# Two pairs of PSUM banks instead of one for the down projection of a mixture-of-experts layer, on 8 cores

## The reference

```
logits = xf @ w_gate                       # [8192, 8]
top_logits, top_idx = top_k(logits, 2)
weights = softmax(top_logits)
for each expert e, its tokens:
    inter = silu(x @ wi_0[e]) * (x @ wi_1[e])   # [tokens, 1024]
    y     = inter @ wo[e]                       # [tokens, 2048]
out = sum over the two experts of a token, weighted
x = x + out
```

## Time and profile before

| | us |
|---|---|
| median of 3 runs | 6443.39 |
| the three runs | 6667.94, 6424.47, 6443.39 |
| the profiled execution, its own time | 6424.47 |
| its span (slowest core, core 7) | 6423.4 |
| spans of the other cores | 6388.9 to 6421.0 |

### The profile page before, as it was taken

One profiled execution on the slowest core, in us unless ns is written; L12 is line 12 of the kernel. 1 busy time (PEld: TensorE's weight loads), 2 busy tenths in 40 slices (PEclk: granted clock), 3 DMA queues, 4 the chain that ended last, 5 costly groups with the idle time before them and its releaser, 6 DMA issues.

```text
span 6423.4 us, 39888 instructions; the slowest of 8 cores (6388.9 to 6423.4 us)
## 1 busy us (share of the span) xinstructions
PE 3070.6 (48%) x13620; PEld 1334.4 (21%) x13620; DVE 887.8 (14%) x1577; ACT 889.7 (14%) x2498; POOL 0.2 (0%) x4
## 2 busy tenths in 40 slices
PE   0002053063063063053437774334448888888887
PEld 0001021021021021021213332111113333333333
DVE  1111101101101101101010002331111111111111
ACT  1001003012022021021041003431110000000000
POOL 0000000000000000000000000000000000000000
PEclk9999575575575575575758885556769999999999
DMA  6764623524524514525310111113332111111111
GB/s 187 246 215 157 222 98 131 201 94 150 197 79 160 199 72 171 182 85 171 137 66 27 53 53 46 40 60 122 120 135 107 66 66 59 59 66 66 61 60 77
DMA packets 181570, 732.71 MB, mean 114 GB/s; under 512 B 13144, under 2 KB 13401, under 8 KB 142460
## 3 DMA queue, kind: packets, MB, share of 16 engines
q10 hardware_dynamic: 73728, 369.13, 16.7%
q1 hardware_dynamic: 107648, 361.03, 16.0%
HBM read 579.10 MB, written 151.01 MB: 114 GB/s over the span
## 4 chain that ended last, share of the span: by engine, by line
PE 43%; DMA 28%; ACT 10%; DVE 10%; issue 7%; ACTq 1%; SPq 0%; DVEq 0%
DMA s_cvf<-wffn_im 19%; PE pb L409 4%; PE pb L411 4%; PE pb L956 4%; DMA s_wqcf<-wqkv 4%; DVE s_cvb L298 4%; PE pb L958 4%; PE pb L912 3%; PE pb L915 3%; PE pb L914 3%; PE pb L913 3%; DMA s_wcg<-wqkvb 3%; PE pb L521 3%; PE pb L523 3%; PE pb L340 2%
## 5 line engine op out<-in xcount | busy, mean ns | idle before, releaser
L409 PE MATMUL pb<-s_wcg,s_lnT 128*128 128x512 bf16 x1536 | 611.6, 398 | 1298.3 <-ACT s_kvst L428 1125.3
L411 PE MATMUL pb<-s_wcg,s_lnT 128*128 128x512 bf16 x1536 | 609.4, 397 | 0.0
L340 PE MATMUL pb<-s_ident,s_lntile 128*128 128x128 bf16 x512 | 135.7, 265 | 979.5 <-ACT s_lntile L330 737.5
L956 PE MATMUL pb<-s_wo,s_inter 128*128 128x512 bf16 x1024 | 396.7, 387 | 237.9 <-DVE s_out L971 208.6
L409 PEld LDWEIGHTS pb<-s_wcg,s_lnT 128*128 128x128 bf16 x1536 | 156.4, 102 | 1505.1 <-issue 1341.2
L298 DVE CAST s_cvb<-s_cvf 128x2048 bf16<-128x2048 f32 x192 | 235.6, 1227 | 1395.8 <-DMA s_cvf<-wffn_im 1395.8
L912 PE MATMUL pb<-s_lnT,s_wi 128*128 128x512 bf16 x1024 | 388.7, 380 | 29.0 <-DMA s_wi<-wall 17.0
L958 PE MATMUL pb<-s_wo,s_inter 128*128 128x512 bf16 x1024 | 396.9, 388 | 0.0
L915 PE MATMUL pb<-s_lnT,s_wi 128*128 128x512 bf16 x1024 | 388.6, 379 | 0.0
L914 PE MATMUL pb<-s_lnT,s_wi 128*128 128x512 bf16 x1024 | 388.6, 379 | 0.0
L913 PE MATMUL pb<-s_lnT,s_wi 128*128 128x512 bf16 x1024 | 388.6, 379 | 0.0
(11 more groups left out here) (124 smaller groups left out, 2850.9 us busy)
## 6 DMA issues: line engine op xcount, KB each, us to landing
s_cvf<-wffn_im ACTq DMA_DIRECT2D x192, 1024.0 KB, 5.9
s_wcg<-wqkvb SPq DMA_DIRECT2D x60, 2048.0 KB, 12.2
wall<-s_cvb ACTq DMA_DIRECT2D x192, 512.0 KB, 2.9
s_wi<-wall ACTq DMA_DIRECT2D x128, 512.0 KB, 4.3
s_wqcf<-wqkv SPq DMA_DIRECT2D x16, 3072.0 KB, 15.6
s_wostr<-woutb SPq DMA_DIRECT2D x64, 512.0 KB, 3.3
s_wo<-wall SPq DMA_DIRECT2D x16, 2048.0 KB, 8.1
wqkvb<-s_wqcb SPq DMA_DIRECT2D x16, 1536.0 KB, 7.0
```

Of the source, the lines that this page charges most:

```text
L340: t.inc(ten.transpose(pbankb(bk, P), s_lntile[:, par * C + ch * P: par * C + (ch + 1) * P], s_ident[:]), pe)
L409: ten.matmul(pbank(2 * pt4, 512), lhs, s_wcg[:, i * KB:i * KB + 512], start=st_, stop=False)
L411: ten.matmul(pbank(2 * pt4 + 1, 512), lhs, s_wcg[:, i * KB + 512:(i + 1) * KB], start=st_, stop=False)
L956: ten.matmul(pbank(ybanks[0], 512), lhs, wosl[:, hc * KB: hc * KB + 512], start=st_, stop=sp)
```

## The change

F2 takes turns between two pairs of banks: 2 and 3 for even `tt`, 6 and 7 for odd `tt`. Ahead of group `tt` PE waits for the evacuation of group `tt - 2`, the last user of the same pair, in place of `tt - 1`. The first two groups of the second half wait for the last two of the first half. The waits for the last silu and the last `s_inter` stand ahead of the second group of an expert too, whose banks 6 and 7 were last used by F1.

```diff
-        ybanks = (2, 3)
         for cs in range(2):
             wpar = wo_dma[(e, cs)][0]
             wosl = s_wo[:, wpar * NHC * KB:(wpar + 1) * NHC * KB]
             t.wait(ten, dGp[wpar], wo_dma[(e, cs)][1])
             for tt in range(NT):
-                if tt == 0 and cs == 0:
+                ybanks = (2, 3) if tt % 2 == 0 else (6, 7)
+                if tt < 2 and cs == 0:
                     t.wait(ten, av, silu_ev[(e, NHC - 1)])
                     t.wait(ten, dv, inter_ev[(e, NHC - 1)])
                     t.wait(ten, dv, inter_ev[(e, NHC - 2)])
-                if (e, tt - 1, cs) in y_evac:
-                    t.wait(ten, dv, y_evac[(e, tt - 1, cs)])
-                elif tt == 0 and cs == 1:
-                    t.wait(ten, dv, y_evac[(e, NT - 1, 0)])
+                if (e, tt - 2, cs) in y_evac:
+                    t.wait(ten, dv, y_evac[(e, tt - 2, cs)])
+                elif tt < 2 and cs == 1:
+                    t.wait(ten, dv, y_evac[(e, NT - 2 + tt, 0)])
```

## The result

| us | before | changed |
|---|---|---|
| median of 13 runs | 6565.96 | 6288.6 |
| shortest and longest | 6424.47, 6898.8 | 6193.69, 6565.86 |
| runs over 50 us above the shortest | 8 of 13 | 8 of 13 |
| median of the other five | 6431.42 | 6208.66 |
| span of the profiled execution | 6423.4 | 6210.7 |

The change makes the kernel faster: ratio 0.9654, 95% interval 0.9607 to 0.9702, which is 223 us. In over half of the executions of either kernel the granted clock of some cores is lowered for a part of the time; this ratio leaves out those in which that costs most, the two medians of 13 leave out none. The forecast of 6206 agrees with the undisturbed executions, the five without it (6194 to 6217). The median of all 13 is 6288.6 and lies outside the range of 6180 to 6240: the prediction missed there.

What follows compares the result with a forecast made beforehand. PE and DVE waiting for each other in turn was taken to bound F2. Boundaries -227.5, clock -1.7 and end +1.2 gave -228.0 us, from 6424.47 to 6196.5; the median was placed at 6206, range 6180 to 6240.

Steps and rivals of the forecast that it cites:

- The price of a boundary, 1.894 us: F2, between groups: 2.11 us between matmul starts less a 0.216 us step, at 120 boundaries, 227.3 us saved.
- Full cover, 1.56 us to spare: F2: evacuation and hand-overs need 2.11 us, have 3.67 us with two bank pairs, so the whole stall goes.
- The rival that DVE becomes the bound: F2: DVE's two instructions take over 3.46 us beside matmuls; at 4.4 us per group, 6320 us; 3%.
- the 16 us in the upper bound: F2: allowance for matmuls losing 9% of each 1.40 us evacuation beside DVE, 128 times; expected 0.
- A free boundary: F2: PE's step into the other banks, with waits long satisfied, costs nothing beyond the usual 0.22 us.
- The clock at the heads: -1.7 us: F2: clock drops after the 8 head gaps stay, the drop inside F2 goes, -1.7 us; bounds 0 and -15.2.
- The end: +1.2: Last 8 output stores, issued 3.46 us apart and taking 3.8 each: 0 to 2.4 us later, taken as 1.2.
- The sum for an execution like the profiled one: Whole kernel: -227.5 - 1.7 + 1.2 = -228.0 us, from 6424.47 to 6196.5 us.
- I place a median of the changed kernel half of that above: Whole kernel: earlier median was 18.9 us above the profiled execution; half of that added gives 6206.
- The rival of the clock: Mixture of experts: denser matmuls lower the granted clock; about 6512 us by the skill's rule, 6722 at 0.72; 10%.
- a clock between the two levels: Changed trace: a granted clock level between the two known ones, listed as a sign that the prediction is wrong.
- The rival of no effect: F2 boundary: something else (weights, DMA) holds PE, so the time stays at about 6440 us; 2%.

Runs made afterwards that it cites:

- experiment 5: Normalised activations set to zero ahead of the first expert, in the changed kernel and the one before: stage 1396.4 and 1620.6 us; changed kernel also rerun unaltered, ratio 0.9646.
- experiments 1 and 2: Against the kernel before: alternating banks with the old wait kept, ratio 0.9978; then the change in experts 0 to 3 alone, ratio 0.980.

## Why the prediction was right, and where it missed

- **The bound.** Right. PE and DVE waited for each other, 120 times.
- **The price of a boundary, 1.894 us.** Right: 228.1 us for 120. Reading it from start to start mattered; the idle times alone would have said 208.6, 19.5 us too few.
- **Full cover, 1.56 us to spare.** Right. Two more instructions on DVE, which take 1.51 us of this, cost F2 0.2 us; four more made DVE the bound. The rival that DVE becomes the bound would have needed that. No step and no evacuation got slower beside the other, so the 16 us in the upper bound were not needed.
- **A free boundary.** Right: 0.22 us.
- **The clock at the heads: -1.7 us.** Mis-sized. The drop inside F2 went, but those at the heads got longer: in the changed kernel the record of core 7 shows 3.4 us at the first two and 6.8 at the other six, where it was 3.4 at each. Its steps inside the groups lost 4.4 us more in all instead of 1.7 less. I had taken the drop after a gap as a fixed price, with bounds that went only one way. It isn't fixed: the gaps at the heads are those of before to 0.03 us, and on core 1 the second has no drop behind it at all.
- **Loads: nothing.** Right, no wait on `s_wo` appeared. **The end: +1.2.** It was 0 on core 7, and at most 0.3 on all cores but core 0.
- **The sum for an execution like the profiled one.** 6196.5 forecast; the five undisturbed ones took 6193.7 to 6217.1. The ratio forecast, 6206 / 6443 = 0.963, lies in the measured interval. That 6206 is within 3 us of the median of those five (6208.66) is in part luck: the sum took off 4 us too much, and the 9.5 us put on for the spread made up for it.
- **The step that failed** is "I place a median of the changed kernel half of that above", a spread of 0 to 18.9 us. The table had one of three runs 243.5 above the shortest, and I took it into a rival instead of the spread. Over 13 runs the median of the changed kernel is 76 us above its profiled execution, and that of before 141 us above its own, because 8 of 13 executions of each were lengthened as in experiment 5. Why one is and the next is not stays open.
- **The rival of the clock.** I gave it 10% and made it a consequence of a denser stage. That condition was wrong: 8 of 13 executions of both kernels lie over 50 us above their shortest. The size was not far off: the longest of the changed kernel is 372 us above its shortest. By the rule of the Trainium skill (TensorE: Matmul & The Clock Gate, Part 1) the estimate was 306 us, for a stage wholly at 13/16. In the traces the level covered about half of the stage at most (782.8 of 1518.6 us), and came in earlier stages too. F1 at 1.00 for 100 us in one profile, on which I relied against it, shows only that this execution was spared. That 0.72 is the lowest mean of a long stretch with matmuls was a misreading, as the earlier trace rows has slices with a clock in the five tenths and PE busy for three. And "a clock between the two levels" stands among my signs of being wrong. The sign came: the changed kernel's own profiled execution had such a level, in the last 33 us of core 3:

```profile
6164.00:6197.00 33.00, 29.71 (x114) 12.12 (x112) 11.28 (x16) 0.00 (x0) 0.00 (x0) 0.82 0.56 235
```

- **The rival of no effect.** It fell with experiments 1 and 2.

## What to carry to other kernels

When two engines alternate on one set of PSUM banks, the price of the alternation is the distance between matmul starts over the boundary less one step, times the boundaries. A second set takes all of it, as long as the other engine's work for a group plus its two hand-overs is shorter than a group and a step: 3.62 of 3.67 us still fitted here. A forecast of the median has to hold the spread of the runs that are already there: if one of three is 4% long, it isn't an outlier until something shows it, and the range has to reach to the shortest plus what such a run adds. And once the large waits are gone, count the small ones with what they do to the clock: 8 gaps of 3.9 us cost 31 us by their length and about 19 more by the matmuls behind them.

## What the runs showed of the hardware that I had not expected

- The granted clock has a level of 0.8125 beside the half and the full one. A 128x512 matmul steps by 0.263 us there, 0.216 at the full clock. In the mixture of experts it appears for 11 to 201 us at a time, and on pairs of cores (2 and 3, 4 and 5, 6 and 7) while the other pair of the die stays at 1.00.
- It depends on the data: with zeros in the mixture of experts none of 12 executions of the kernel before is over 140 us above the shortest, with the real data on the same chip 11 of 23 are.
- Gaps of 3.41 us between matmuls, in the kernel before with twice the evacuation, put the clock at half for 138 us of the stage; gaps of 1.89 us hardly ever did. Behind gaps of 3.93 us it was at half for 3.4 us, for 6.8 or not at all.
- DVE's evacuation at f32 takes 742 to 751 ns whether PE stands still or writes other banks at its full rate.
